# Layer 0's summing stage: the first rest of a row is made on VectorE instead of GpSimd

## The chip, the cores and the metric

The kernel runs on one core of one Trainium2 chip. The metric is the device time of one execution in microseconds (us), the median over several executions. A core has five engines that run in parallel, each with its own instruction stream, and tell each other by semaphores: TensorE (PE, its weight loads PEld), VectorE (DVE), ScalarE (ACT), GpSimd (POOL) and SyncE (SP, here only a DMA queue).

## The reference

Two graph layers over 12,500 nodes with 64 features and 400,000 edges, with a residual and a layer norm after each. The change lies in the neighbourhood sum of layer 0:

```
row = concatenate([src, loop]); col = concatenate([dst, loop]); w = concatenate([edge_weight, ones])
deg = segment_sum(w, row); dinv = where(deg > 0, deg ** -0.5, 0)
agg = segment_sum((dinv[row] * w * dinv[col])[:, None] * x[col], row)
x = layernorm(x + agg @ W.T + b)
```

Layer 1 (messages by a two-layer perceptron over each edge, summed by dst, then a GRU update) is not touched.

## The kernel before

The program is a row of stages, each a block in which every engine has its own stream; a stage starts when all engines have left the one before. For layer 0 an earlier stage (`move_rows`) sorts 400,000 weighted rows in DRAM by source node, so that each group of 640 rows (`GE`, 5 rows for each of 128 partitions) falls into one window of 128 nodes. A moved row has 65 float32 words (`ROW`): 64 features and, in the last, the lane of its node within the window.

The stage of this case is `sum_moved`: it adds each group into its window's sums. There are `NQ` = 723 groups, handled in turns of eight (`SL` = 8 buffer slots). `over_groups` writes the first turn out, loops over the turns after it (the loop is opened at line 97), and writes a last turn of three groups out. At the head of each turn VectorE loads 11 registers (8 + `LAG`) with window numbers from the table `q_tab` (line 957). For each group q:

- SyncE loads the 162.5 KB of rows into slot s as soon as TensorE is through with the group eight before (line 920).
- TensorE multiplies in bfloat16, and a float32 value goes through it in three parts: its high half, the high half of what is left (`left`), and the rest of that in bfloat16 (`rest`). GpSimd makes `left` = row less its high half (line 928), as soon as the rows are in. VectorE makes `rest` = `left` less the high half of `left` (line 976).
- A one-hot matrix of 128 lanes stands for each of the 5 rows of a partition. VectorE makes three of them by a comparison (line 973), ScalarE two by two activations each (lines 941 and 934).
- TensorE does 15 matmuls, 5 rows by 3 parts, into one PSUM slot (line 994).
- VectorE adds the PSUM slot of group q - 3 (`LAG` = 3) to the sums of its window (line 965).

VectorE's order within a group is: comparison (973), wait for `left_made`, `rest` (976), then `add` (965). GpSimd does nothing else in this stage. Nothing but the order of the code and the semaphores sets the order of the work; there is no planner.

Lines of this document's profile that end in q (DVEq) are instructions that an engine's sequencer handles itself: register arithmetic, branches, loads of registers.

Of the kernel before, what the change touches and what calls it, by code (L numbers as in the profile page):

```python
# [23 lines left out]
ALU, ACT = mybir.AluOpType, mybir.ActivationFunctionType  # L24
# [3 lines left out]
N, E, D, HD = 12500, 400000, 64, 128  # L28
# [3 lines left out]
G = 5  # L32
# [5 lines left out]
NQ = (E + NW * (GE - 1)) // GE + 1  # L38
# [5 lines left out]
LAG = 3  # L44
# [9 lines left out]
def wait(eng, sem, value):  # L54

    if not isinstance(value, int) or value > 0:
        eng.wait_ge(sem, value)


def wait_alone(eng, sem, value, passed):  # L60


    eng.wait_ge(sem, value)
    eng.sem_inc(passed, 1)
# [24 lines left out]
def over_groups(eng, n, body, load=None, slots=S):  # L89


    def turn(i, count):
        loaded = load(i * slots, count) if load else None
        for s in range(count):
            body(i * slots + s, s, i, loaded)
    turn(0, slots)
    with eng.Fori(1, n // slots) as i:
        turn(i, slots)
    if n % slots:
        turn(n // slots, n % slots)  # L100
# [7 lines left out]
def is_first(g):  # L108
    return isinstance(g, int) and g == 0


def cols(t, start, size):
    return t[:, bass.ds(start, size)]


def high_halves(ap):

    return ap.bitcast(BF16).rearrange("p (a b) -> p a b", b=2)[:, :, 1]


def split3(ap, n):
    return ap.rearrange("p (a b) -> p a b", a=n)


def program(nc, x, src, dst, w, attr, W, b, W1, b1, W2, b2, W_ih, b_ih, W_hh, b_hh, out, places, table, moved, tile_base, a_dram, x1_dram, x1T_dram, attr9, c_dram, b_dram, rel_table, base_dram):
    with ExitStack() as ctx:
        def sb(name, shape, dt):
# [58 lines left out]
        move_rows(nc, dst, lane_row, node_id, before_bf, ones_bf, src_hi, src_lo, weight,  # L186
                  step_tab, tables, tile_base, moved)
        sum_moved(nc, lane_row, ones, q_tab, tables, moved, acc)
        nodes(nc, ident, eps, weight, xs, dinv, acc, W_T, b_b, W1_T, b1_b, tables, a_dram, b_dram, x1_dram, x1T_dram)
        counts_row = tables[0:1, 0:2 * NB_ROWS].bitcast(F32)  # L190
# [693 lines left out]
def sum_moved(nc, lane_row, ones, q_tab, tables, moved, acc):  # L884

    SL = 8  # L890
    VT = 3
    with ExitStack() as ctx:
        def sb(name, shape, dt):
            return ctx.enter_context(nc.sbuf_tensor(name, shape, dt))

        def sem(name):
            return ctx.enter_context(nc.semaphore(name))


        rows = split3(tables[:, 0:2 * SL * G * ROW].bitcast(F32), SL)  # L900
        left = split3(tables[:, 2 * SL * G * ROW:2 * SL * G * (ROW + D)].bitcast(F32), SL)
        rest = sb("rows_rest", [P, SL, G * D], BF16)
        hot = sb("lane_hot", [P, SL, G, P], BF16)
        away = sb("lanes_away", [P, SL, G - VT, P], BF16)
        ps = ctx.enter_context(nc.psum_tensor("ps_moved", [P, SL, 512], F32))
        rows_in = [sem(f"moved_in{s}") for s in range(SL)]
        left_made, hot_made, away_made, act_hot_made = sem("left_made"), sem("lane_hot_made"), sem("away_made"), sem("act_hot_made")
        summed, added, cleared = sem("rows_summed"), sem("sums_added"), sem("sums_cleared")
        passed = sem("sum_moved_passed")
        block = ctx.enter_context(nc.Block())  # L910

        def high_rows(s):
            return split3(high_halves(rows[:, s, :]), G)[:, :, 0:D]

        @block.sync
        def _(sp):
            def body(q, s, use, _):

                wait(sp, summed, q - (SL - 1))
                sp.dma_start(rows[:, s, :], moved[bass.ds(q * GE, GE), :].rearrange("(p r) c -> p (r c)", p=P)).then_inc(rows_in[s], 16)  # L920
            over_groups(sp, NQ, body, slots=SL)

        @block.gpsimd
        def _(pool):
            def body(q, s, use, _):

                wait_alone(pool, rows_in[s], use * 16 + 16, passed)
                pool.tensor_tensor(split3(left[:, s, :], G), split3(rows[:, s, :], G)[:, :, 0:D], high_rows(s), ALU.subtract).then_inc(left_made, 1)  # L928
            over_groups(pool, NQ, body, slots=SL)

        @block.scalar
        def _(act):
            def near(s):
                act.activation(hot[:, s, VT:, :], away[:, s, :, :], ACT.Relu, bias=ones[:, 0:1], scale=-1.0).then_inc(act_hot_made, 1)

            def body(q, s, use, _):
                act.wait_ge(rows_in[s], use * 16 + 16)

                wait(act, act_hot_made, q - (SL - 1))
                for j in range(VT, G):  # L940
                    last = act.activation(away[:, s, j - VT, :], lane_row[:, :], ACT.Abs,
                                          bias=rows[:, s, j * ROW + D:j * ROW + D + 1], scale=-1.0)
                last.then_inc(away_made, 1)
                if not is_first(q):
                    act.wait_ge(away_made, q)
                    near((s - 1) % SL)
            over_groups(act, NQ, body, slots=SL)
            act.wait_ge(away_made, NQ)
            near((NQ - 1) % SL)

        @block.vector
        def _(dve):
            regs = [dve.alloc_register(f"sum_dve{i}") for i in range(SL + LAG)]

            def load(q0, count):

                dve.load(regs[0:count + LAG], q_tab[0:1, bass.ds(q0, count + LAG)])
                return [dve.snap(x).with_bounds(min_val=0, max_val=NW - 1) for x in regs[0:count + LAG]]

            def add(q, s, win):  # L960
                dve.wait_ge(summed, q + 1)

                wait(dve, added, q)
                here = cols(acc, win * D, D)
                dve.tensor_tensor(here, here, ps[:, s, 0:D], ALU.add).then_inc(added, 1)  # L965

            dve.memset(acc, 0.0).then_inc(cleared, 1)
            dve.wait_ge(cleared, 1)

            def body(q, s, use, wins):  # L970

                dve.wait_ge(rows_in[s], use * 16 + 16)
                dve.tensor_tensor(hot[:, s, 0:VT, :], lane_row[:, :].unsqueeze(1).to_broadcast([P, VT, P]),
                                  split3(rows[:, s, :], G)[:, 0:VT, D:D + 1].to_broadcast([P, VT, P]), ALU.is_equal)
                dve.wait_ge(left_made, q + 1)
                dve.tensor_tensor(rest[:, s, :], left[:, s, :], high_halves(left[:, s, :]), ALU.subtract).then_inc(hot_made, 1)
                if not (isinstance(q, int) and q < LAG):
                    add(q - LAG, (s - LAG) % SL, wins[s])
            over_groups(dve, NQ, body, load, slots=SL)
            wins = load(NQ - LAG, LAG)  # L980
            for i in range(LAG):
                add(NQ - LAG + i, (NQ - LAG + i) % SL, wins[LAG + i])

        @block.tensor
        def _(pe):
            def body(q, s, use, _):
                pe.wait_ge(hot_made, q + 1)
                pe.wait_ge(act_hot_made, q + 1)

                wait(pe, added, q - (SL - 1))  # L990
                for j in range(G):
                    parts = high_rows(s)[:, j, :], high_halves(left[:, s, :])[:, j * D:(j + 1) * D], rest[:, s, j * D:(j + 1) * D]
                    for i, part in enumerate(parts):
                        last = pe.matmul(ps[:, s, 0:D], hot[:, s, j, :], part, start=(i == j == 0), stop=(i == 2 and j == G - 1))  # L994
                last.then_inc(summed, 1)
            over_groups(pe, NQ, body, slots=SL)
# [637 lines left out]
```

## Time and profile before

| | |
|---|---|
| median of 3 runs | 11367.97 us (11355.69 to 11370.47) |
| profiled execution, span | 11347.2 us |
| median less that span | 20.8 us |
| this stage, from VectorE's first comparison to its last addition | 1083.96 us, 9.6% of the span |
| busy over the whole span | PE 65%, DVE 53%, ACT 20%, POOL 67% |
| busy in this stage | PE 707.0, DVE 1020.3, ACT 779.7, POOL 590.6 us |

The profile is of one execution. A row of a timeline gives the start in us, the length in us, the engine, the line, the operation with what it writes and reads, and in brackets the idle time before it with what ended it. Instructions of one engine overlap a little at their ends, so the distance from start to start says what an instruction costs, and it is less than its length.

### The profile page before, as it was taken

To read this page: it belongs to the slowest core of one execution; us is meant where nothing else is said; L and a number is where in the kernel's file an instruction comes from. 1 tells how busy PE (TensorE), PEld (TensorE's weight loads), DVE (VectorE), ACT (ScalarE), POOL (GpSimd) and SP (SyncE) were. 2 spreads that over 40 slices of the span, in tenths; PEclk is the share of its full clock that TensorE was granted. 3 is DMA by queue.
4 is the path that set the end of the run, shared out by engine and by line. 5 is a ranking of instruction groups with operands and counts; after the bars stand their busy time and mean duration, and the time that the engine had idled before them with its cause. 6 is when DMAs were issued, how large, how long until landed. Compare 5 with 4: busy or idle time off the path is not lost. (4 is left out here: it accounts for less than half of the span.)

```text
span 11347.2 us, 232069 instructions
## 1 busy us (share of the span) xinstructions
PE 7401.2 (65%) x59805; PEld 5933.9 (52%) x59806; DVE 5957.9 (53%) x18225; ACT 2279.0 (20%) x7946; POOL 7635.7 (67%) x7653
## 2 busy tenths in 40 slices
PE   4777733333333333333366665999999999999999
PEld 3666621111122222222255554888888888888885
DVE  6999953333333333333499985444444444444443
ACT  1000001111111111111277751111111111111111
POOL 3666637777777777777755531777777777777771
PEclk9999965555555555555555555555555555555555
DMA  6500022222222222222244432333333333333321
GB/s 246 235 0 0 0 50 78 77 77 79 77 77 77 77 77 77 77 77 77 75 110 111 110 94 79 89 86 86 86 86 86 86 85 86 86 86 86 86 82 34
DMA packets 627617, 950.45 MB, mean 84 GB/s; under 512 B 202831, under 2 KB 381213, under 8 KB 627329
## 3 DMA queue, kind: packets, MB, share of 16 engines
q1 hardware_dynamic: 427582, 640.84, 19.8%
q0 software_dynamic: 200000, 309.20, 9.6%
q8 instruction: 15, 0.25, 0.0%
q14 instruction: 20, 0.16, 0.0%
HBM read 690.33 MB, written 259.09 MB: 84 GB/s over the span
## 5 line engine op out<-in xcount | busy, mean ns | idle before, releaser
L1251 POOL DMA_INDIRECT tables<-a_half,src_i x3125 | 3069.1, 982 | 1271.1 <-issue 945.2
L853 POOL DMA_INDIRECT moved<-tables,place x3125 | 3067.7, 982 | 1083.8 <-issue 934.9
L815 PE MATMUL ps_rows<-tables,dst_hot 128*128 x10830 | 808.2, 240 | 2625.0 <-ACT tables L844 1513.1
L815 PEld LDWEIGHTS ps_rows<-tables,dst_hot 128*128 128x128 bf16 x10830 | 668.9, 125 | 2968.9 <-issue 2926.4
L1372 PE MATMUL ps_msum<-tables,src_cols 128*128 128x64 f32 x6250 | 1498.0, 427 | 0.0
L1372 PEld LDWEIGHTS ps_msum<-tables,src_cols 128*128 128x128 f32 x6250 | 1380.5, 329 | 136.6 <-issue 136.6
L1276 DVE TENSOR_TENSOR src_cols<-ps_pre,tables 128x640 f32<-128x640 f32 x625 | 515.1, 824 | 1736.3 <-DMA tables<-a_half,src_i 1732.6
L843 ACT ACTIVATE tables<-ps_rows,edge_cols 128x64 f32<-128x64 f32 x3125 | 707.3, 318 | 3357.0 <-DMA moved<-tables,place 3220.5
L779 DVE CAST place<-place_f 128x5 int32<-128x5 f32 x625 | 109.9, 176 | 2110.4 <-DMA moved<-tables,place 2107.0
L564 POOL TENSOR_TENSOR tables<-hi_hot,edge_cols 128x490 f32<-128x490 bf16 x625 | 853.6, 1366 | 472.3 <-DVE hi_hot L573 472.3
L1353 ACT ACTIVATE src_cols<-src_cols 128x640 f32<-128x640 f32 x625 | 460.5, 737 | 3511.0 <-DVE src_cols L1276 3447.0
L1399 PE MATMUL ps_pre<-b_rows,tables 64*128 64x128 bf16 x9375 | 1110.1, 309 | 0.0
L655 PE MATMUL ps_degrees<-tables,lo_hot 128*128 128x128 f32 x6250 | 865.5, 286 | 346.8 <-POOL tables L564 346.8
L1399 PEld LDWEIGHTS ps_pre<-b_rows,tables 64*128 64x128 bf16 x9375 | 945.0, 142 | 122.7 <-issue 122.7
L655 PEld LDWEIGHTS ps_degrees<-tables,lo_hot 128*128 128x128 f32 x6250 | 746.4, 192 | 399.5 <-POOL tables L564 399.5
L994 PE MATMUL ps_moved<-tables,lane_hot 128*128 128x64 bf16 x7230 | 668.7, 241 | 420.2 <-DVE sums L965 319.2
L928 POOL TENSOR_TENSOR tables<-tables 128x320 f32<-128x320 f32 x723 | 596.1, 825 | 492.9 <-DMA tables<-moved 492.6
L1370 PE MATMUL ps_msum<-tables,ones 128*1 128x64 f32 x6250 | 765.6, 308 | 248.5 <-ACT src_cols L1353 247.6
L573 DVE TENSOR_TENSOR hi_hot<-lane_row,src_cols 128x490 bf16<-128x490 bf16 x625 | 913.7, 1462 | 8.8 <-PEq L354 8.8
L994 PEld LDWEIGHTS ps_moved<-tables,lane_hot 128*128 128x128 bf16 x7230 | 556.6, 127 | 532.5 <-DVE sums L965 417.9
L1261 DVE TENSOR_SCALAR tables<-lane_row,base_col,edge_cols 128x64 f32<-128x64 bf16 x3125 | 773.7, 327 | 10.7 <-issue 1.4
L1370 PEld LDWEIGHTS ps_msum<-tables,ones 128*1 128x1 f32 x6250 | 602.0, 118 | 281.2 <-issue 279.9
(229 smaller groups left out, 10100.8 us busy)
## 6 DMA issues: line engine op xcount, KB each, us to landing
dst_rows<-in_dst SPq DMA_DIRECT2D x625, 320.0 KB
tables<-moved SPq DMA_DIRECT2D x723, 162.5 KB, 2.2
moved<-sums SPq DMA_DIRECT2D x180, 650.0 KB, 9.0
m_dst_rows<-in_dst SPq DMA_DIRECT2D x625, 160.0 KB
moved<-tables,place POOLq DMA_INDIRECT x3125
tables<-a_half,src_i POOLq DMA_INDIRECT x3125
b_rows<-b_half SPq DMA_DIRECT2D x625, 48.0 KB
base_rows<-tile_bases SPq DMA_DIRECT2D x625, 2.9 KB
```

The source lines that it names most:

```text
L564: pool.tensor_tensor(hi_weight[:, s, :, 0:NW], hi_hot[:, s, :, :], cols(weight, g * G, G).unsqueeze(2).to_broadcast([P, G, NW]), ALU.mult) ...
L573: dve.tensor_tensor(hi_hot[:, s, :, :], lane_row[:, 0:NW].unsqueeze(1).to_broadcast([P, G, NW]), cols(src_hi, g * G, G).unsqueeze(2).to_br ...
L655: last = pe.matmul(ps[:, 0:P], lo_hot[:, s, j, :], hi_weight[:, s, j, :], start=first and j == 0, stop=last_one and j == G - 1, skip_group ...
L815: last = pe.matmul(ps_rows[:, h, j * D:(j + 1) * D], dst_hot[:, slot, j * P:(j + 1) * P], cols(parts, win * (3 * D) + i * D, D), start=beg ...
L843: act.activation(rows[:, s, j, 0:D], ps_rows[:, s % 2, j * D:(j + 1) * D], ACT.Copy, scale=cols(weight, g * G + j, 1))
L853: pool.indirect_dma_start(out=moved[:, :], out_offset=bass.IndirectOffsetOnAxis(ap=place[:, s, j:j + 1], axis=0), in_=rows[:, s, j, :], in ...
L994: last = pe.matmul(ps[:, s, 0:D], hot[:, s, j, :], part, start=(i == j == 0), stop=(i == 2 and j == G - 1))
L1251: pool.indirect_dma_start(out=a_rows[:, s, j, :], out_offset=None, in_=a_dram[:, :], in_offset=bass.IndirectOffsetOnAxis(ap=src_i[:, s, j: ...
L1261: last = dve.tensor_scalar(node_hot[:, slot, j, :], lane_row[:, 0:C], start, cols(dst_f, g * G + j, 1), ALU.add, ALU.is_equal)
L1370: pe.matmul(ps_sum[0:1, slot, C:2 * C], ones[:, 0:1], node_hot[:, slot, j, :], start=(j == 0), stop=(j == G - 1))
L1372: last = pe.matmul(ps_sum[:, slot, 0:C], hidden[:, h if slot == 2 else slot, j, :], node_hot[:, slot, j, :], start=(j == 0), stop=(j == G ...
L1399: last = pe.matmul(ps_pre[:, h, j * HD:(j + 1) * HD], dst_hot[:, slot, j * P:(j + 1) * P], b_rows[:, b_slot, i * HD:(i + 1) * HD], start=F ...
```

## The change

VectorE makes `left` itself, directly behind the comparison, and now adds group q - 3 between `left` and `rest`. GpSimd's part of the stage is gone, and with it the semaphore `passed`. The wait for `left_made` stays ahead of `rest`, but what it waits for is now an instruction of VectorE's own.

```diff
-        passed = sem("sum_moved_passed")
...
-        @block.gpsimd
-        def _(pool):
-            def body(q, s, use, _):
-
-                wait_alone(pool, rows_in[s], use * 16 + 16, passed)
-                pool.tensor_tensor(split3(left[:, s, :], G), split3(rows[:, s, :], G)[:, :, 0:D], high_rows(s), ALU.subtract).then_inc(left_made, 1)
-            over_groups(pool, NQ, body, slots=SL)
...
                 dve.wait_ge(rows_in[s], use * 16 + 16)
                 dve.tensor_tensor(hot[:, s, 0:VT, :], lane_row[:, :].unsqueeze(1).to_broadcast([P, VT, P]),
                                   split3(rows[:, s, :], G)[:, 0:VT, D:D + 1].to_broadcast([P, VT, P]), ALU.is_equal)
+                dve.tensor_tensor(split3(left[:, s, :], G), split3(rows[:, s, :], G)[:, :, 0:D], high_rows(s), ALU.subtract).then_inc(left_made, 1)
+                if not (isinstance(q, int) and q < LAG):
+                    add(q - LAG, (s - LAG) % SL, wins[s])
                 dve.wait_ge(left_made, q + 1)
                 dve.tensor_tensor(rest[:, s, :], left[:, s, :], high_halves(left[:, s, :]), ALU.subtract).then_inc(hot_made, 1)
-                if not (isinstance(q, int) and q < LAG):
-                    add(q - LAG, (s - LAG) % SL, wins[s])
```

## Rows read from the trace of the kernel before

**Rows 1.** The page: busy time of each engine; busy tenths in 40 slices.
```profile
PE 7401.2 (65%) x59805; PEld 5933.9 (52%) x59806; DVE 5957.9 (53%) x18225; ACT 2279.0 (20%) x7946; POOL 7635.7 (67%) x7653
...
DVE  6999953333333333333499985444444444444443
```
**Rows 2.** Windows view of the stage: length; busy of PE, PEld, DVE, ACT, POOL; clock; DMA.
```profile
5641.65:6725.61 1083.96, 707.01 (x10845) 595.05 (x10845) 1020.31 (x2169) 779.74 (x2152) 590.63 (x716) 0.50 0.41 110
```
**Rows 3.** Groups by line in the same window.
```profile
L928 POOL TENSOR_TENSOR tables<-tables 128x320 f32<-128x320 f32 x716 | 591.3, 826 | 486.4 <-DMA tables<-moved 486.1
L973 DVE TENSOR_TENSOR lane_hot<-lane_row,tables 128x384 bf16<-128x384 bf16 x723 | 582.8, 806 | 64.4 <-issue 64.4
...
L976 DVE TENSOR_TENSOR rows_rest<-tables 128x320 bf16<-128x320 f32 x723 | 446.4, 617 | 0.0
...
L965 DVE TENSOR_TENSOR sums<-sums,ps_moved 128x64 f32 x723 | 149.9, 207 | 0.8 <-DVE sums L965 0.8
```
**Rows 4.** Waits in the same window: total us, times, longest.
```profile
ACT lanes_away L941 <- DMA tables<-moved: 292.8, 590, 4.0
...
DVE lane_hot L973 <- issue: 64.4, 91, 1.6
```
**Rows 5.** Timeline of VectorE, a group of the first turn, and the next's start.
```profile
5645.28 0.55 DVE L973 TENSOR_TENSOR lane_hot<-lane_row,tables 128x384 bf16<-128x384 bf16 x1
5645.75 0.48 DVE L976 TENSOR_TENSOR rows_rest<-tables 128x320 bf16<-128x320 f32 x1
5646.15 0.21 DVE L965 TENSOR_TENSOR sums<-sums,ps_moved 128x64 f32 x1
5646.28 0.55 DVE L973 TENSOR_TENSOR lane_hot<-lane_row,tables 128x384 bf16<-128x384 bf16 x1
```
**Rows 6.** Timeline of GpSimd around the first turn.
```profile
5637.60 4.13 POOL L928 TENSOR_TENSOR tables<-tables 128x320 f32<-128x320 f32 x6 [0.30 <-DMA tables<-moved]
5647.51 2.29 POOL L928 TENSOR_TENSOR tables<-tables 128x320 f32<-128x320 f32 x2 [5.78 <-DMA tables<-moved]
```
**Rows 7.** Timeline of VectorE, last group of a turn and start of the next turn.
```profile
6202.06 0.94 DVE L973 TENSOR_TENSOR lane_hot<-lane_row,tables 128x384 bf16<-128x384 bf16 x1
6202.92 1.00 DVE L976 TENSOR_TENSOR rows_rest<-tables 128x320 bf16<-128x320 f32 x1
6203.84 0.21 DVE L965 TENSOR_TENSOR sums<-sums,ps_moved 128x64 f32 x1
6204.49 0.94 DVE L973 TENSOR_TENSOR lane_hot<-lane_row,tables 128x384 bf16<-128x384 bf16 x1 [0.44 <-issue]
```
**Rows 8.** Timeline of GpSimd over the same groups.
```profile
6202.83 0.74 POOL L928 TENSOR_TENSOR tables<-tables 128x320 f32<-128x320 f32 x1 [0.25 <-DMA tables<-moved]
6204.30 0.72 POOL L928 TENSOR_TENSOR tables<-tables 128x320 f32<-128x320 f32 x1 [0.73 <-DMA tables<-moved]
```
**Rows 9.** Lines 957 (all, then 6202:6205) and 97: ns min/median/max, first and last start.
```profile
L957 DVEq TENSOR_LOAD <-q_tab x92: 825/1292/1309, 5640.1 to 6723.3; - x92
...
L957 DVEq TENSOR_LOAD <-q_tab x1: 1308/1308/1308, 6202.8 to 6202.8; - x1
...
L97 DVEq ALU_OP  x1: 40/40/40, 6202.4 to 6202.4; - x1
```
**Rows 10.** Timeline of VectorE at the stage's start.
```profile
5634.81 5.29 DVE L967 MEMSET sums<- 128x6272 f32 x1 [28.90 <-issue]
5641.65 0.56 DVE L973 TENSOR_TENSOR lane_hot<-lane_row,tables 128x384 bf16<-128x384 bf16 x1 [1.56 <-issue]
```
**Rows 11.** Another stage: timeline row at line 1276, and line 1268's sequencer row behind it.
```profile
8004.89 0.82 DVE L1276 TENSOR_TENSOR src_cols<-ps_pre,tables 128x640 f32<-128x640 f32 x1 [3.94 <-DMA tables<-a_half,src_i]
...
L1268 DVEq FUSED_REGOPS  x1: 53/53/53, 8005.0 to 8005.0; - x1
```
**Rows 12.** Timeline of VectorE where each instruction waits for the one before.
```profile
1579.24 3.43 DVE L679 CAST tables<-sums 128x6272 bf16<-128x6272 f32 x1
1582.70 6.69 DVE L680 TENSOR_TENSOR tables<-sums,tables 128x6272 f32<-128x6272 f32 x1
```

## The prediction

> **What bounds the kernel now.** I read the page first: over the whole span no engine is busy all the time, and VectorE's slices show a band of nines at slices 20 to 23, higher than before and after it [rows 1]. That band is the changed stage, 1083.96 us long in the windows view: VectorE is busy 1020.3 us of it, TensorE 707.0, ScalarE 779.7 and GpSimd 590.6 [rows 2]. The view of waits confirms who leads: VectorE never waits for another engine or a DMA there, only 64.4 us for "issue", its own sequencer; ScalarE waits for the rows' DMA, 292.8 us, because it has run ahead as far as the loads allow [rows 4]. So VectorE's stream sets the stage, at 1083.96 / 723 = 1.499 us for a group and 11.99 us for a turn of eight.
>
> What makes up the 1.499? The grouped view gives VectorE 0.806, 0.617 and 0.207 us [rows 3], but these means hide two populations. In the first turn, at 5645.28, a group runs comparison 0.55, rest 0.48, addition 0.21 long, and from start to start 0.47 + 0.40 + 0.13 = 1.00 us [rows 5]. GpSimd had then subtracted for the first eight groups ahead of time and idled for 5.78 us until 5647.51 [rows 6], while ScalarE, TensorE and the loads were at work. Later, at 6202.06, the same comparison takes 0.94 and the same rest 1.00 [rows 7], and GpSimd's subtractions, 0.72 to 0.74 long, lie over exactly these two stretches, at 6202.83 and 6204.30 [rows 8]. So one GpSimd subtraction holds VectorE up by some 0.4 to 0.5 us; over the stage the mean group pays (0.806 - 0.55) + (0.617 - 0.48) = 0.39 us for it. That leaves 1.499 - 1.00 - 0.39 = 0.11 us a group, or 0.87 a turn, for the head of the turn, where the sequencer goes round the loop and loads 11 registers in 1.31 us [rows 9].
>
> **The change part by part.**
>
> GpSimd's subtraction goes: 591.3 us off an engine that is not the bound, worth nothing by itself, but the 0.39 us a group that it costs VectorE goes too. I take the clean group of [rows 5] for all three old instructions: 1.00 us. GpSimd's removed wait and count release nobody else; its queue issues no DMA in this stage.
>
> VectorE's new subtraction: 320 float32 elements from a float32 and a strided bfloat16 operand. The nearest row is `rest`, same count and same second operand: 0.40 us from start to start [rows 5]. It can't be less than that, the fastest of the kind; at most I give it the full length, 0.48, if rows that are 65 words apart cost it something. I take 0.40, because `rest` has the same element count. 0.40 for 0.39: the swap itself is nearly nothing, 723 x 0.01 = 7 us.
>
> On those rows the Trainium skill has a price ("Vector Engine (DVE) Microarchitecture Reference", the SBUF access granule): a port is slower where its runs of adjacent words start on an odd word, 1.30 instead of 1.054 ns per column for runs of two. Every second row here starts on an odd word; by that figure the sum would grow by at most 723 x 320 x 0.246 ns / 2 = 28 us, an estimate; no row of before shows such a read on VectorE.
>
> The wait for `left_made` is now for VectorE's own instruction. The dependent pair at line 680 starts 0.03 us after its producer's end (1579.24 + 3.43 = 1582.67, start 1582.70) [rows 12]. Here `left` ends 0.48 after its start and the wait is over at 0.51; the addition put in between occupies VectorE until 0.40 + 0.13 = 0.53. So inside a turn the wait costs nothing; at worst, if `rest` can't start before the addition has ended (0.61 + 0.03), 0.11. Inside a turn the group is 0.47 + 0.40 + 0.13 + 0.40 = 1.40 us.
>
> At the end of a turn the same wait costs much. Before, nothing in VectorE's stream has to wait, so its sequencer is ahead of its datapath: at 6202.06 the last comparison starts; at 6202.4 the loop's first register instruction is already handled and at 6202.8 the load of 11 registers begins, though `rest` has not started (6202.92) and the addition comes at 6203.84 [rows 7, 9]. The next comparison starts at 6204.49, that is 2.43 after the last one's start and 2.1 after the loop's first instruction. With the change the sequencer stands at `rest` until `left` is done, and everything queued behind it in the stream, the branch, the load, the next comparison, waits too. That a wait holds the sequencer is seen at line 1276: it waits 3.94 us for a DMA, starts at 8004.89, and the sequencer's next work for line 1268 is at 8005.0, behind it [rows 11]. So after the change the 2.1 us begin with the start of `rest`; with 0.05 for getting past it, 2.15 us from `rest` to the next comparison where 0.40 would do. Bounds: from below the stage's start, where a wait, the load and the first comparison follow each other without a branch, 5640.10 to 5641.65 = 1.55 us [rows 10]; from above the whole 2.43. I take 2.15, since it is this loop's own chain.
>
> TensorE gets `rest` 0.53 us later behind the comparison, once and not per group, and works 707.0 / 723 = 0.98 us a group, ScalarE 779.7 / 723 = 1.08: both still fit under 1.40. The addition of group q - 3 now stands ahead of `rest`; its product was released more than two groups, over 2.8 us, before, so it does not wait. SyncE's loads follow TensorE's ends with eight slots; VectorE never waits for them at 1.00 us a group either [rows 4, 5].
>
> **The sum.** A turn: 7 x 1.40 + (0.47 + 0.53 + 2.15) = 9.80 + 3.15 = 12.95 us, against 11.99. There are 92 register loads, one ahead of the first turn and one ahead of the last additions, so 90 turn ends [rows 9]: 90 x 12.95 = 1165.5. The last three groups and the three closing additions with their load take some 6 us. The stage: 1171.6, against 1083.96: +88 us. The profiled span would be 11347.2 + 88 = 11435; the median of the runs lies 20.8 above the span, 11367.97 + 88 = 11456 us, 0.77% slower.
>
> **The rivals.**
>
> *The wait does not hold the sequencer* and the run-ahead stays. For it speaks that a satisfied wait lets it run ahead today; against it [rows 11]. The last group of a turn then lasts 2.43 from its comparison, as before, or 2.03 if a queue of four instructions lets the sequencer run from the `rest` before: a turn of 11.83 to 12.23, -14 to +22 us in all, middle 11372: not slower. It decides at 11.99 - 9.80 = 2.19 us from the last comparison of a turn to the next; I forecast 3.15. The Trainium skill leans this way ("VectorE: DVE Perf Modes", the DRAIN you can't avoid): of chained instructions it says "the semaphore costs nothing extra here". Inside the turn the trace agrees (0.03 us); of a loop's end the page says nothing.
>
> *The strided subtraction or the wait is dearer in every group.* At 0.48 instead of 0.40: +58 us more, 11514. At 0.11 of waiting for the addition: +80, 11536. Against it: `rest` reads the same strided halves at 0.40.
>
> *VectorE's slow instructions are not GpSimd's doing* but the loads'. Then 0.39 stays and the group gains 0.40 on top: 723 x 0.39 = 282 us more, 11738. Against it: in the first turn loads and ScalarE were running and VectorE was clean [rows 5, 6].
>
> **How the numbers follow.** Forecast 0.73, run-ahead stays 0.13, dearer in every group 0.11, not GpSimd's doing 0.03. The forecast's own range comes from the turn's end: 1.55 would take 90 x 0.60 = 54 us off, 2.43 adds 25: 11402 to 11481. Up to 11520 takes in most of the dearer case, and down to 11395 leaves out most of the run-ahead case, so 11395 to 11520 holds 8 in 10. Within 0.2% (23 us, about what a measurement of this kernel tells from no change) lies most of the run-ahead case: 0.10. Faster by more 0.05, slower by more 0.85.
>
> **What would show it.** The comparison's and rest's mean lengths should fall to 0.55 and 0.48 (wrong: the means stay near 0.81 and 0.62). The new subtraction should be 0.48 long. Inside a turn comparison to comparison should be 1.40. VectorE's "issue" idle in the stage should rise from 64.4 to about 90 x 1.67 = 150 us, now ahead of a comparison that follows a `rest`; line 957's loads should start about 0.5 us behind the start of `rest`. If that idle stays near 64 and the time near 11370 to 11390, the run-ahead survived. If ScalarE or a DMA releases a VectorE wait, I have missed a bound.

## The result and the profile after

The changed kernel takes 11456.02 us (median of 4, 11454.10 to 11458.05) against 11367.38 for the kernel before: ratio 1.0078, 95% interval 1.0064 to 1.0092. It is 89 us slower; the forecast was 88. That the two agree within 1 us is partly luck: the interval spans some 73 to 105 us, and the medians of the kernel before, 11353 to 11367 us over this document, differ by 14.

The profiled spans differ by more, 11453.9 - 11347.2 = 106.7 us. Only 85.6 of it lies in the stage; the rest lies in stages that the change doesn't touch. The profiled execution of before was quick there (its span is 20.2 us under the median of 11367.38, that of after 2.1), and over all kernels below, whose code up to this stage differs in nothing but the constant LAG, the stage starts anywhere from 5638 to 5655 us. So below I compare stages, and each median with that of the kernel before taken beside it, which is why that number varies.

The windows view of the stage (length; busy of PE, PEld, DVE, ACT, POOL; clock; DMA), answering [rows 2]:

```profile
5654.91:6824.50 1169.59, 708.39 (x10845) 596.10 (x10845) 1023.50 (x2892) 782.76 (x2153) 0.00 (x0) 0.50 0.39 102
```

VectorE does 723 instructions more and is busy for nearly the same time, 1023.5 against 1020.3 us, but the stage is 85.6 us longer. The groups by line, answering [rows 3], say why its busy time hardly changed:

```profile
L964 DVE TENSOR_TENSOR lane_hot<-lane_row,tables 128x384 bf16<-128x384 bf16 x723 | 397.1, 549 | 146.4 <-issue 146.4
...
L966 DVE TENSOR_TENSOR tables<-tables 128x320 f32<-128x320 f32 x723 | 348.0, 481 | 0.0
L970 DVE TENSOR_TENSOR rows_rest<-tables 128x320 bf16<-128x320 f32 x723 | 347.7, 481 | 0.1
L956 DVE TENSOR_TENSOR sums<-sums,ps_moved 128x64 f32 x723 | 152.0, 210 | 1.1 <-issue 0.7 <-PE ps_moved L986 0.2 <-DVE sums L956 0.2
```

The comparison fell from a mean of 806 to 549 ns and `rest` from 617 to 481, together 393, which pays for the new subtraction (line 966: 481 long, 0.40 us from its start to the next one's). What grew is idle time put down to "issue", 64.4 to 146.4 us: 82 us, nearly all of the loss. The timeline of VectorE at the end of a turn shows where it sits, answering [rows 7]:

```profile
6206.63 0.55 DVE L964 TENSOR_TENSOR lane_hot<-lane_row,tables 128x384 bf16<-128x384 bf16 x1
...
6208.03 0.55 DVE L964 TENSOR_TENSOR lane_hot<-lane_row,tables 128x384 bf16<-128x384 bf16 x1
6208.50 0.48 DVE L966 TENSOR_TENSOR tables<-tables 128x320 f32<-128x320 f32 x1
6208.90 0.21 DVE L956 TENSOR_TENSOR sums<-sums,ps_moved 128x64 f32 x1
6209.03 0.48 DVE L970 TENSOR_TENSOR rows_rest<-tables 128x320 bf16<-128x320 f32 x1
6211.13 0.56 DVE L964 TENSOR_TENSOR lane_hot<-lane_row,tables 128x384 bf16<-128x384 bf16 x1 [1.61 <-issue]
```

Inside a turn 1.40 us from comparison to comparison; at its end 3.10, with 2.10 from the start of `rest` to the next comparison. The sequencer's own rows for the loop (line 97) and for the load of the window numbers (line 948 now) in this stretch, answering [rows 9]:

```profile
L97 DVEq ALU_OP  x1: 40/40/40, 6209.0 to 6209.0; - x1
```
```profile
L948 DVEq TENSOR_LOAD <-q_tab x1: 1283/1283/1283, 6209.5 to 6209.5; - x1
```

The loop's first instruction comes with the start of `rest`, not ahead of it as before. The load runs from 6209.5 to 6210.8; `rest` has ended by then (6209.03 + 0.48), so the datapath, the part of VectorE that computes, has nothing to do.

### The profile page after: what moved, and what is told of

It reads as the page before. It is cut to its first block and busy times, and to the rows that moved or that the text cites. A ratio compares the mean times of both kernels' runs of the same rounds, so it can differ in the third digit from the quotient of the medians.

```text
span 11453.9 us, 231078 instructions
## 1 busy us (share of the span) xinstructions
PE 7403.1 (65%) x59805; PEld 5935.8 (52%) x59806; DVE 5970.8 (52%) x18948; ACT 2284.5 (20%) x7946; POOL 7060.7 (62%) x6930
## 5 line engine op out<-in xcount | busy, mean ns | idle before, releaser
L986 PE MATMUL ps_moved<-rows_rest,lane_hot 128*128 128x64 bf16 x3615 | 637.6, 242 | 0.0
```

## The experiments

All times from start to start of the comparison are taken from VectorE's timeline over the whole stage: a median for inside a turn (632 of the 722 distances) and one for the 90 turn ends. For the kernel before they are 1.39 (mean 1.37) and 2.42, for the changed one 1.40 and 3.10.

The same reading can be made at each of the 89 turn ends inside the loop. The medians, with the loop's first register instruction (line 97) as the point at which the sequencer gets to the branch:

| kernel | sequencer at the branch, behind the start of the last comparison | from there to the next VectorE instruction | turn end |
|---|---|---|---|
| before | 0.31 | 2.11 | 2.42 |
| changed | 1.00 | 2.11 | 3.10 |
| the order alone | -0.37 | 2.11 | 1.73 |
| own wait in the last group | 0.91 | 2.11 | 3.02 |
| own wait in the fourth group | 0.31 | 2.11 | 2.42 |
| wait directly behind `left` | 1.20 | 2.11 | 3.31 |
| `rest` one group later | 0.31 | 2.11 | 2.42 |

So the chain of branch, load and register work is the same 2.11 us in all seven, and the turn ends differ only by when the sequencer gets to it. In the changed kernel that is 0.05 us behind the end of the last `left`; in the kernel before it is 0.24 behind the end of the addition before the last comparison. The experiments test what moves this point.

My theory after the result: a wait at which VectorE's sequencer stands for a young product, here its own `left`, keeps it from running ahead, and this costs where the branch and the 1.3 us load stand behind it; the swap of GpSimd's interference for one more instruction is nearly even. Rivals: the order of the instructions, the length of the subtraction, a fixed price for each own wait, and a source for VectorE's slow instructions other than GpSimd.

**The order alone.** The kernel before with the addition ahead of `rest`; GpSimd still makes `left`.

```diff
+                if not (isinstance(q, int) and q < LAG):
+                    add(q - LAG, (s - LAG) % SL, wins[s])
                 dve.wait_ge(left_made, q + 1)
                 dve.tensor_tensor(rest...).then_inc(hot_made, 1)
-                if not (isinstance(q, int) and q < LAG):
-                    add(q - LAG, (s - LAG) % SL, wins[s])
```

> GpSimd still makes left; only VectorE's order is that of the change (comparison, addition, rest). Theory (what costs is a wait for VectorE's own instruction at the end of a turn): the wait for left_made is long over here, so the sequencer isn't held by it; it is still held by the addition's wait for the addition before it, now 0.4 us earlier in the group. The median lies within 0.3% of the kernel before, 11335 to 11400 us, and VectorE's issue idle in the stage stays near 64 us. Rival (the order, with rest last in the group and the turn ending on it, costs by itself): near the changed kernel, 11440 to 11460 us.

Measured: 11347.29 against 11354.02, ratio 0.9995 (0.9985 to 1.0004); the stage 1076.2 us, idle for "issue" 50.6. The order is not to blame. There is a surprise in it: the end of a turn shrank to 1.73, while inside a turn the mean rose to 1.45. The lengths explain the second: comparison and `rest` together are 1.43 us long in the mean (743 + 689 ns) where they were 1.42 (806 + 617), so GpSimd holds VectorE up as long as before. But in the kernel before 0.63 us of it a turn fell into the last group, beside the 2.11 us chain of the sequencer, and here only 0.09; the rest now falls inside the turn. So what the turn end gained, 62 us in all, the groups inside mostly lost again (54).

**One own wait in each turn.** The kernel before, with `rest` made to wait for the comparison just ahead of it in one group of eight: the last (s == 7), or the fourth (s == 3).

```diff
-                dve.tensor_tensor(hot...)
+                last = dve.tensor_tensor(hot...)
+                if s == 7:
+                    last.then_inc(compared, 1)
+                    dve.wait_ge(compared, use + 1)
                 dve.wait_ge(left_made, q + 1)
```

> The kernel before with one thing added: in the last group of each turn rest also waits for the comparison just before it on VectorE. 90 waits in all. Theory (such a wait holds the sequencer, and the loop's branch and the load of 11 registers then lie bare): rest starts at the comparison's end instead of 0.08 us ahead of it, and the next comparison comes about 2.4 us behind that rest: 3.0 to 3.3 us from comparison to comparison at the end of a turn instead of 2.43; 90 times 0.5 to 0.9 us: 45 to 80 us more, 11412 to 11448 us. Rival (the wait doesn't hold the sequencer): 90 times 0.1 us, 11370 to 11380 us.

> The kernel before with the added wait of e7_own_wait_slot7, but in the fourth group of a turn instead of the last. Theory (such a wait costs much only where the loop's branch and load stand behind it): each of the 90 waits costs 0.1 to 0.15 us for the start of rest behind the comparison's end, 5 to 15 us in all, no change that can be told (within 0.2% of before). Rival (a wait for an own instruction costs its 0.5 us wherever it stands): 0.4% slower, as with the wait in the last group.

Measured: in the last group 11403.34 against 11354.02, ratio 1.0043 (1.0027 to 1.0058), the stage 1138.1 us; in the fourth 11372.56 against 11353.48, ratio 1.0018 (1.0009 to 1.0028), the stage 1100.8 us. The same 90 waits cost 54 us of stage ahead of the loop's end and 17 in the middle of the turn. The first is within the 45 to 80 us that I gave it, though the median lies under 11412 us, which was counted from a slower median of before; the second is a little more than the 5 to 15, and clear of no change. The turn end went from a mean of 2.41 to 3.17 with the wait in the last group and stayed at 2.41 with the wait in the fourth, where that group itself went from 1.01 to 1.31. The groups without a wait changed too, by 10 to 15 us in all, because GpSimd's work fell elsewhere. Timeline of VectorE with the wait in the last group; `rest` starts 0.67 behind the comparison instead of 0.47 or 0.86, and the next comparison is 3.02 behind the one before:

```profile
6201.88 0.54 DVE L974 TENSOR_TENSOR lane_hot<-lane_row,tables 128x384 bf16<-128x384 bf16 x1
6202.55 0.80 DVE L980 TENSOR_TENSOR rows_rest<-tables 128x320 bf16<-128x320 f32 x1
6203.28 0.21 DVE L966 TENSOR_TENSOR sums<-sums,ps_moved 128x64 f32 x1
6204.90 0.56 DVE L974 TENSOR_TENSOR lane_hot<-lane_row,tables 128x384 bf16<-128x384 bf16 x1 [1.41 <-issue]
```

**GpSimd's subtraction given back, for nothing.** The changed kernel, and GpSimd subtracts the same rows into a tile that nobody reads.

```diff
+        @block.gpsimd
+        def _(pool):
+            def body(q, s, use, _):
+                wait(pool, spare_made, q - 1)
+                wait_alone(pool, rows_in[s], use * 16 + 16, passed)
+                pool.tensor_tensor(split3(spare[:, s % 2, :], G), ..., high_rows(s), ALU.subtract).then_inc(spare_made, 1)
...
+                wait(sp, spare_made, q - (SL - 1))
```

> The changed kernel, with GpSimd subtracting the same rows once more into a spare tile that nobody reads; only the loads wait for it, eight groups later. Theory (each GpSimd subtraction holds VectorE up by 0.4 to 0.5 us where it falls on a two-input instruction): the means of VectorE's comparison, left and rest rise together by 0.35 to 0.45 us a group, less what falls into the idle time at a turn's end: 200 to 310 us more than the changed kernel, 11650 to 11765 us. Rival (VectorE's slow instructions came from the row loads or ScalarE): no change against the changed kernel, 11456 us within 0.2%.

Measured: 11750.58 against 11354.02, ratio 1.0349 (1.0333 to 1.0365); the changed kernel is at 1.0078, so GpSimd's useless work costs 0.0271 of 11354, 308 us, or 311 by the stages (1480.9 against 1169.6): 0.43 us a group. Groups by line in the stage:

```profile
L923 POOL TENSOR_TENSOR spare<-tables 128x320 f32<-128x320 f32 x716 | 668.7, 934 | 801.9 <-DMA tables<-moved 719.4 <-issue 82.3
...
L979 DVE TENSOR_TENSOR tables<-tables 128x320 f32<-128x320 f32 x723 | 536.9, 743 | 0.0
...
L977 DVE TENSOR_TENSOR lane_hot<-lane_row,tables 128x384 bf16<-128x384 bf16 x723 | 461.5, 638 | 146.5 <-issue 146.5
...
L983 DVE TENSOR_TENSOR rows_rest<-tables 128x320 bf16<-128x320 f32 x723 | 399.1, 552 | 0.1
```

All three long instructions of VectorE grew (by 262, 89 and 71 ns, 0.42 us together), the idle time did not. This is at the upper end of what I expected. The rival of the loads and ScalarE falls.

**`rest` one group later.** The changed kernel, but the `rest` made behind `left` of group q is that of group q - 1.

```diff
+            def make_rest(q, s):
+                dve.wait_ge(left_made, q + 1)
+                dve.tensor_tensor(rest[:, s, :], left[:, s, :], ..., ALU.subtract).then_inc(hot_made, 1)
...
+                if not is_first(q):
+                    make_rest(q - 1, (s - 1) % SL)
                 if not (isinstance(q, int) and q < LAG):
                     add(q - LAG, (s - LAG) % SL, wins[s])
-                dve.wait_ge(left_made, q + 1)
-                dve.tensor_tensor(rest...).then_inc(hot_made, 1)
```

> The changed kernel with rest of group q-1 made behind left of group q, ahead of the addition: the wait for left_made is over a whole group before. The same four instructions a group. Theory (the wait for left just made holds the sequencer): what holds it now is only the addition's wait for the addition before it, over 0.1 us behind the start of the comparison, so a turn is 7 x 1.40 + 2.43 = 12.23 us instead of 12.95: 90 x 0.72 = 65 us less than the changed kernel, 11391 us, within 11370 to 11400; VectorE's issue idle falls to 80 to 95 us. Rival (the time is in the subtraction's own length or in the order): no change against the changed kernel, 11440 to 11470 us.

Measured: 11364.72 against 11354.02, ratio 1.0008 (0.9999 to 1.0017), so 0.7% off the changed kernel; the stage 1107.7 us, inside a turn 1.40, at its end 2.42, idle 85.1. The same four instructions of the same lengths; `left` is now a group old when it is waited for, and the addition ends the group instead of `rest`. The second can't be what helps, since with the order alone the turn's end was shorter with `rest` last (1.73 against 2.42). This undoes 62 of the 86 us, 3 fewer than I expected, and the 24 that stay are the swap inside the turns (1.37 to 1.40).

**The wait directly behind `left`.** The changed kernel with the addition last again.

```diff
-                if not (isinstance(q, int) and q < LAG):
-                    add(q - LAG, (s - LAG) % SL, wins[s])
                 dve.wait_ge(left_made, q + 1)
                 dve.tensor_tensor(rest...).then_inc(hot_made, 1)
+                if not (isinstance(q, int) and q < LAG):
+                    add(q - LAG, (s - LAG) % SL, wins[s])
```

> The changed kernel with the addition behind rest again, so that rest directly follows the left it waits for. Theory: inside a turn nothing covers left's end, 0.48 + 0.03 us from left to rest and then 0.40 and 0.13, so 1.51 us a group instead of 1.40; at the end of a turn the addition's register work comes behind rest too, 3.3 to 3.4 us instead of 3.10. The stage 1240 to 1270 us, 1.4% to 1.7% slower than the kernel before. Rival (a wait for an own instruction costs nothing between instructions): the stage near 1170 us, as in the changed kernel, 0.8% slower than before.

Measured: 11549.15 against 11366.20, ratio 1.0160 (1.0144 to 1.0176); the stage 1265.3 us, inside a turn 1.53, at its end 3.31. The addition between `left` and `rest` was worth 0.12 us a group: it is what hides the wait inside a turn.

**No load at the turn's head.** The registers are loaded once; every turn adds into the windows of the first turn, which leaves out the choice of the windows.

```diff
-            over_groups(dve, NQ, body, load, slots=SL)
-            wins = load(NQ - LAG, LAG)
+            fixed = load(0, SL)
+            over_groups(dve, NQ, body, lambda q0, count: fixed, slots=SL)
+            wins = fixed
```

> The changed kernel without the load of window numbers at the head of each turn: the registers are loaded once and every turn adds into the windows of the first; that part of the computation is left out. Theory: the end of a turn consists of the wait's hold, the branch and the load, and the load with its register work is 1.5 of its 3.10 us: 1.5 to 1.7 us remain from comparison to comparison, 90 times 1.4 to 1.6 us less: the stage 1025 to 1045 us, 0.35% to 0.55% faster than the kernel before. Rival (the load hides beside the datapath and the hold is all): the end of a turn stays above 2.6 us, the stage above 1120 us, slower than before.

Measured: 11331.58 against 11366.20, ratio 0.9969 (0.9957 to 0.9981); the stage 1022.2 us, the end of a turn 1.46, both slightly under the ranges I gave; the kernel is 0.31% faster than before, where I gave at least 0.35%. Of the 1.70 us that a turn's end costs beyond a group in the changed kernel, 1.64 are the load and the register work behind it; the branch alone leaves 0.06.

**A turn of sixteen for VectorE**, with 19 registers in each load (`slots=2 * SL`, slot `s % SL`).

> The changed kernel with VectorE's turn twice as long: sixteen groups for each branch and load, which then loads 19 registers. Theory: half as many bare turn ends, each longer by 8 registers at about 0.09 us (0.82 us for 6 and 1.29 for 11): 3.8 to 4.0 us from comparison to comparison at an end, 45 of them, 1.40 inside: the stage 1125 to 1140 us, 0.3% less than the changed kernel and 0.4% to 0.5% slower than before. Rival (the cost lies in every group): the stage stays near 1170 us.

Measured: 11422.84 against 11366.20, ratio 1.0049 (1.0034 to 1.0065); the stage 1125.6 us, 44 less than the changed kernel; idle for "issue" 107.0 in 46 pieces. The end of a turn is 3.85, and the load 1.80 us where it was 1.29.

**The addition first, and then one group later.** As with `rest` one group later, and the addition moved to the head of the group; in the second kernel also LAG = 4.

```diff
             def body(q, s, use, wins):
+                if not (isinstance(q, int) and q < LAG):
+                    add(q - LAG, (s - LAG) % SL, wins[s])
                 dve.wait_ge(rows_in[s], use * 16 + 16)
...
                     make_rest(q - 1, (s - 1) % SL)
-                if not (isinstance(q, int) and q < LAG):
-                    add(q - LAG, (s - LAG) % SL, wins[s])
```
```diff
-LAG = 3
+LAG = 4
```

> The changed kernel, with rest of group q-1 behind left of group q and the addition at the head of the group: addition, comparison, left, rest of the group before. Now neither the wait for left nor the addition's wait for the addition before it is for anything younger than a group. Theory (each wait for VectorE's own young instruction holds the sequencer, and what is held at the end of a turn lies bare): the sequencer runs ahead as far as its queue allows and hides most of the branch and the load; from comparison to comparison 1.40 us inside a turn and 1.4 to 1.8 at its end, the stage 1012 to 1050 us: 30 to 72 us less than the kernel before in the same call, 0.3% to 0.6% faster. Rival (the 2.4 us at the end of a turn are a fixed price of branch and load, whatever the order): 2.4 us at the end, the stage near 1108 us, 0.1% to 0.3% slower than before.

Measured: 11384.41 against 11366.20, ratio 1.0015 (1.0006 to 1.0024), the stage 1112.4 us, the turn's end 2.43. My expectation failed: the rival's number came out. TensorE's timeline and the sequencer's row for line 956 suggest why:

```profile
6202.64 0.29 PE L991 MATMUL ps_moved<-tables,lane_hot 128*128 128x64 bf16 x2
6202.74 0.24 PE L991 MATMUL ps_moved<-rows_rest,lane_hot 128*128 128x64 bf16 x1
```
```profile
L956 DVEq FUSED_REGOPS  x1: 57/57/57, 6203.0 to 6203.0; - x1
```

The addition's wait is passed at 6203.0, when TensorE's product of that group is just done (6202.74 + 0.24 = 6202.98): with `rest` a group later and the addition earlier, three groups' distance had been used up, and now TensorE held VectorE's sequencer. That is a reading of one stretch; the products and rows around it read the same (ends 6201.58, 6204.39 and 6205.84, rows at 6201.6, 6204.4 and 6205.9). The second kernel tests it.

> As e5_rest_late_add_first, with LAG = 4: the addition at the head of the group is for the group four before. In e5 the sequencer passed the addition's wait for TensorE's product only as that product ended, about a group and a half behind the rest it was made from, so VectorE's sequencer was held by TensorE. Theory (any young product that the sequencer stands at holds it, from whatever engine): a group more of distance frees it; it is then held only by the wait for the addition before, and the end of a turn is 1.5 to 2.0 us from comparison to comparison instead of 2.43: the stage 1025 to 1075 us, 0.1% to 0.5% faster than before. Rival (2.4 us is the price of branch and load, or a short queue keeps the sequencer from running further ahead): the end stays at 2.4 us, the stage at 1110 us, 0.15% slower than before, as in e5.

Measured: 11305.60 against 11353.48, ratio 0.9960 (0.9946 to 0.9973), the stage 1034.3 us, inside a turn 1.40, at its end 1.59. This kernel beats both, by 0.4% and 1.2%. But LAG = 4 changed two things, not one. Timeline of VectorE at a turn's end:

```profile
6201.15 0.55 DVE L970 TENSOR_TENSOR lane_hot<-lane_row,tables 128x384 bf16<-128x384 bf16 x1
6201.62 0.48 DVE L972 TENSOR_TENSOR tables<-tables 128x320 f32<-128x320 f32 x1
6202.02 0.48 DVE L963 TENSOR_TENSOR rows_rest<-tables 128x320 bf16<-128x320 f32 x1
6202.60 0.22 DVE L956 TENSOR_TENSOR sums<-sums,ps_moved 128x64 f32 x1
6202.74 0.55 DVE L970 TENSOR_TENSOR lane_hot<-lane_row,tables 128x384 bf16<-128x384 bf16 x1
```

The sequencer's rows for the load (the whole stage) and for the loop at this turn end:

```profile
L948 DVEq TENSOR_LOAD <-q_tab x92: 847/851/1860, 5643.0 to 6674.6; - x92
```
```profile
L97 DVEq ALU_OP  x1: 40/40/40, 6200.7 to 6200.7; - x1
```

The load, now of 12 registers, takes 0.85 us where the load of 11 took 1.29. Of the 0.84 us by which the turn end is shorter than with LAG = 3, 0.44 are this shorter load. The other 0.40 are the sequencer's: it gets to the branch 0.40 ahead of the start of the last comparison, where with LAG = 3 it came level with it. So the freer sequencer accounts for about half of the gain. At the load's old length the end would be 2.03 us, just outside what I gave it, and the median near 11345, an estimate from 90 x 0.44 = 40 us; that would be hardly ahead of the kernel before. Why 12 registers load faster than 11 no run here shows. The load's time doesn't simply follow the number: the closing load of 8 in this kernel took 1.86 us.

Of branch and load 0.2 us are left bare. What holds the sequencer now is again one of VectorE's own products: the `left` of the group before ends at 6201.62 - 1.40 + 0.48 = 6200.70, the loop's first register instruction comes at 6200.7, and over the 89 ends the median distance is 0.05 us.

**The same with a turn of sixteen.**

> As e10_lag4_add_first, with VectorE's turn of sixteen groups and a load of 20 registers. Theory: half as many turn ends, each longer by about 0.8 us of load, 2.3 to 2.8 us from comparison to comparison at an end: the stage within 15 us of e10's. Rival (the queue doesn't let the sequencer run ahead): ends of 3.2 us, the stage near 1095 us.

Measured: 11327.36 against 11353.48, ratio 0.9977 (0.9968 to 0.9986), the stage 1053.3 us, so 19 us behind the kernel with turns of eight, outside the 15 I gave it; the end of a turn is 2.21, a little under my 2.3 to 2.8. The longer load (20 registers, 1.35 us) no longer hides: 31.5 us of "issue" idle ahead of line 956. Where almost nothing was bare, fewer and longer loads came out worse.

## Why the prediction was right

*The bound.* VectorE's stream set the stage before and after: ScalarE's wait for rows grew from 292.8 to 373.4 us, and VectorE has no wait for another engine but 0.2 us at the very end. Right.

*The swap, 0.39 off and 0.40 on.* Right as a price for a group: inside a turn the mean went from 1.37 to 1.40 us. But that is 23 us over the stage, not the 7 us of 723 x 0.01: GpSimd's price inside a turn was 0.36, and the mean of 0.39 has the dearer last groups in it. The sum didn't suffer, since it was built from turns of 7 x 1.40. The clean lengths of [rows 5] (0.55, 0.48, 0.21) are what every group now has, and the given-back GpSimd work costs 0.43 a group. One reading of rows was loose: the GpSimd subtraction at 6202.83 lies over `rest` [rows 7, 8], but the one at 6204.30 lies over the comparison of the next turn; the slow comparison at 6202.06 met the one before, which began at 6201.62 and ended at 6202.58. Where the price falls depends on the order (0.36 inside a turn before, 0.45 with the order alone), but its sum over the stage hardly does, 286 and 292 us by the lengths.

*The subtraction at 0.40.* Right: from 6208.50 to 6208.90, 481 ns long, like `rest`. The Trainium skill's figure for runs that start on an odd word ("Vector Engine (DVE) Microarchitecture Reference", the SBUF access granule) would have added up to 28 us; the trace shows nothing of it for runs of 64 words.

*No cost of the wait inside a turn, behind the addition.* Right, 0.13 from the addition to `rest`; and with the addition taken away, 0.12 a group appears, as worked out.

*2.15 us from `rest` to the next comparison.* Measured 2.10, so 3.10 instead of 3.15 a turn's last group. The stage came out at 1169.6 instead of 1171.6: 632 x (1.405 - 1.368) = 23 us inside the turns, and 90 x (3.092 - 2.407) = 62 at their ends, in means.

*One step was wrong in its words:* "Before, nothing in VectorE's stream has to wait". The sum took the 2.43 us as measured, so it didn't suffer. But those 2.43 had a cause: each addition waits for the addition before it, at the end of a group, so the sequencer was held there too, until 0.12 us behind the start of the last comparison. With `rest` last and the addition in the middle the end was 1.73. I had taken the old turn end for the loop's price, and 0.69 of the 1.02 us that it costs beyond a group were the same fault as the new one. For the same reason my "run-ahead stays" rival was priced at what the order before gives, 2.43.

*The rival of the run-ahead*, with the rule that semaphores between chained VectorE instructions cost nothing ("VectorE: DVE Perf Modes", the DRAIN you can't avoid, in the Trainium skill), fell at the turn's end: one own wait in a turn cost 54 us in the stage. In the middle of a turn the runs agree with it only roughly: 17 us for 90 waits.

Not settled: the last order with LAG = 4 was not run with GpSimd at work, nor the kernel before with a load of 12 registers, so how much of the 0.4% comes from GpSimd's absence is open.

## What to carry to other kernels

On VectorE the sequencer had to run ahead of the datapath to hide the loop's branch and register load. A wait for something the engine itself had just been given stopped that (0.6 us at each turn end), even where the datapath saw hardly a gap from it. Put a loop's end behind waits for products that are old already, count the distance for every engine in the ring, and look for the fault in a profile as "issue" idle ahead of the first instruction of a turn, and in when the sequencer's row of the loop comes. When a constant is changed for such a test, see whether the load has changed with it. Work taken off GpSimd gave VectorE back 0.43 us a group here, and the instruction that replaced it cost 0.40: moving the work was worth nothing by itself.

## What the runs showed of the hardware

In these traces the two-input instructions of GpSimd and VectorE take turns and don't slow each other evenly. In the kernel with the useless GpSimd work, the timeline of the two engines around one collision:

```profile
6200.90 0.54 DVE L977 TENSOR_TENSOR lane_hot<-lane_row,tables 128x384 bf16<-128x384 bf16 x1
6200.99 1.03 POOL L923 TENSOR_TENSOR spare<-tables 128x320 f32<-128x320 f32 x1 [0.89 <-DMA tables<-moved]
...
6201.37 1.00 DVE L979 TENSOR_TENSOR tables<-tables 128x320 f32<-128x320 f32 x1
6202.29 0.21 DVE L969 TENSOR_TENSOR sums<-sums,ps_moved 128x64 f32 x1
```

The comparison was under way when GpSimd started and kept its 0.54 us; GpSimd's instruction took 1.03 instead of the 0.72 of a free one, 0.3 more. VectorE's next one started while GpSimd's ran and ended at 6202.37, 0.35 behind GpSimd's end at 6202.02, so most of its 0.48 us of work came only then. In the kernel before, `rest` at 6202.92 [rows 7] ended at 6203.92, likewise 0.35 behind GpSimd's end at 6203.57 [rows 8]. Over the whole stage of the kernel before, the median comparison that began under a GpSimd instruction ended 0.41 behind it and the median `rest` 0.35, and those that had begun first kept their 0.55 and 0.48 us. The addition that reads PSUM kept its 0.21 us in all kernels, but it was always short, so that it is exempt isn't shown.
